# Folding the first feed-forward's low-rank factors into its weight tiles on chip

## The reference, cut to what matters

```python
def lora(x, w, a, b):            # rank 16, SCALING = 2.0
    return x @ w.T + (x @ a.T) @ b.T * 2.0
g = silu(lora(h, w1, A1, B1)) * lora(h, w3, A3, B3)    # w1, w3: 1376 x 512
x = x + lora(g, w2, A2, B2)                            # w2: 512 x 1376
```

## Time and profile before

| | |
|---|---|
| median of 3 runs | 2982.11 us (2981.08 to 2985.95) |
| the profiled execution's own time | 2981.35 us |
| its span on the core | 2979.5 us |
| PE busy | 2886.9 us, 97% of the span |
| DVE, ACT, POOL busy | 1705.7, 1121.6, 991.4 us |
| the stage (from 868 to 1102 us) | 234 us |

### The profile page before, as it was taken

How to read it: one execution, slowest core, us unless ns; L and a number is a source line. 1 busy time by engine, 2 the same in 40 slices (tenths; PEclk the granted TensorE clock), 3 DMA queues, 4 the chain that set the end, 5 groups by cost and what they waited for, 6 DMA issues and landing times.

```text
span 2979.5 us, 47771 instructions
## 1 busy us (share of the span) xinstructions
PE 2886.9 (97%) x16134; PEld 2433.1 (82%) x16134; DVE 1705.7 (57%) x3462; ACT 1121.6 (38%) x3635; POOL 991.4 (33%) x830
## 2 busy tenths in 40 slices
PE   7999999999999998899999999999999999999999
PEld 6888888888888865577778888888778888888787
DVE  6545544445462249988766666666664444445644
ACT  4322222222242237732354444444443333333432
POOL 3433343423313226644333322332232333332221
PEclk9999999999999999999999999999999999999999
DMA  3111111111112111011111101110021111110111
GB/s 121 46 50 41 40 39 41 48 41 44 42 36 57 34 43 30 27 43 39 37 40 36 31 26 32 35 35 18 26 60 33 36 35 35 35 35 22 46 50 46
DMA packets 68613, 120.09 MB, mean 40 GB/s; under 512 B 8681, under 2 KB 14185, under 8 KB 68113
## 3 DMA queue, kind: packets, MB, share of 16 engines
q1 hardware_dynamic: 68498, 118.60, 13.4%
HBM read 116.41 MB, written 2.10 MB: 40 GB/s over the span
## 4 chain that ended last, share of the span: by engine, by line
PE 86%; DVE 8%; issue 3%; ACT 2%; POOL 1%; DMA 0%; DVEq 0%; SPq 0%; ACTq 0%; POOLq 0%
PE proj L397 40%; PE outp L397 24%; PE heado L1015 6%; PE score L974 6%; PE turn L1001 3%; PE score L397 2%; PE proj L413 1%; PE proj L941 1%; DVE blockmax L1715 1%; DVE picks L1725 1%; PE outp L1995 0%; DVE firstmax L1723 0%; PE turn L924 0%; PE proj L1958 0%; DVE acts L1705 0%
## 5 line engine op out<-in xcount | busy, mean ns | idle before, releaser
L397 PE MATMUL outp<-w_out,acts 128*128 128x512 f32 x3288 | 843.2, 400 | 13.0 <-DVE x L1700 3.9
L397 PE MATMUL proj<-xnT,w_in 128*128 128x512 f32 x3192 | 757.2, 392 | 1.3 <-ACT big L1079 1.3
L397 PEld LDWEIGHTS outp<-w_out,acts 128*128 128x128 f32 x3288 | 594.1, 188 | 144.1 <-DVE x L1700 13.0
L397 PEld LDWEIGHTS proj<-xnT,w_in 128*128 128x128 f32 x3192 | 592.6, 188 | 124.7 <-issue 1.5
L397 PE MATMUL proj<-ctxT,w_kv 128*128 128x512 f32 x1536 | 366.0, 394 | 19.8 <-POOL w_kv L731 18.6
L729 POOL TENSOR_TENSOR w_out<-ring,consts 128x512 fp32r<-128x512 f32 x96 | 102.4, 1066 | 820.9 <-PE outp L397 820.9
L397 PEld LDWEIGHTS proj<-ctxT,w_kv 128*128 128x128 f32 x1536 | 286.6, 189 | 79.1 <-issue 18.6
L1306 DVE TENSOR_TENSOR x<-x,outp 128x512 f32<-128x512 f32 x360 | 244.7, 685 | 182.2 <-PE outp L397 179.1
L1082 DVE COPY big<-proj 128x512 f32<-128x512 f32 x136 | 93.6, 688 | 343.6 <-PE proj L397 339.3
L1079 ACT ACTIVATE big<-proj 128x512 f32<-128x512 f32 x136 | 81.4, 598 | 476.4 <-PE proj L397 469.7
L729 POOL TENSOR_TENSOR w_kv<-ring,consts 128x512 fp32r<-128x512 f32 x93 | 98.0, 1053 | 464.0 <-DMA ring<-in_L_wk 445.6
(11 more groups left out here) (330 smaller groups left out, 4022.7 us busy)
## 6 DMA issues: line engine op xcount, KB each, us to landing
ring<-in_L_wq SPq DMA_DIRECT2D x96, 256.0 KB, 2.7
ring<-in_L_wo SPq DMA_DIRECT2D x96, 256.0 KB, 2.7
ring<-in_F_in SPq DMA_DIRECT2D x52, 256.0 KB, 2.7
ring<-in_L_wk SPq DMA_DIRECT2D x48, 256.0 KB, 2.7
ring<-in_L_wv SPq DMA_DIRECT2D x48, 256.0 KB, 3.4
ring<-in_F_out SPq DMA_DIRECT2D x41, 256.0 KB, 2.6
x<-in_x SPq DMA_DIRECT2D x2, 1024.0 KB, 8.4
big<-in_ctxT SPq DMA_DIRECT2D x4, 512.0 KB, 8.0
```

What stands on the lines that cost most here:

```text
L397: mm = pe.matmul(bank_ap, w_ap(a, c), rhs(b, c), start=first and c == 0 and n == 0, stop=last and c == chunks - 1 and n == len(PASSES) - 1)
```

## The change: what it does

The low-rank products with activations go away. Instead the product of the factors themselves is made on PE, B1 A1 and B3 A3 for an `in` or `in2` tile and A2 B2 for an `out` tile. DVE adds twice that to the raw tile in its ring slot (`merge`), and ACT and POOL round and split the sum as they did the raw tile. The factors stand four times on 64 partitions (high, low, high, high against high, high, low, ...), so that one matmul over 64 rows gives all three passes and one more; `fold_in` makes both input tiles of the next chunk, with eight matmuls of 64 rows and 128 columns that alternate between partitions 0 to 63 and 64 to 127 and between two banks; `fold_out` makes the `out` tile's with one of 64 rows and 512 columns.

```diff
+        def fold_bank(n):
+            return proj[n] if n < 2 else ln_banks[n % 2]
+
+        def fold_in(pe, c):
+            m, n = F0.events, F0.tile(0, c, 0)
+            for k in range(2):
+                m.wait(pe, "merged", n + k - 1 if n else 0)
+            for i in range(DC):
+                for k in range(2):
+                    rows = slice(64 * k, 64 * k + 64)
+                    mm = pe.matmul(fold_bank(n + k)[:, i * P:(i + 1) * P], low_in[rows, i * P:(i + 1) * P],
+                                   low_b[rows, 0, c * P:(c + 1) * P], start=True, stop=True)
+                    if i == DC - 1:
+                        mm.then_inc(m["folded"], 1)
+
+        def fold_out(pe, c):
+            m, n = F0.events, F0.tile(0, c, 2)
+            if c == 0:
+                m.wait(pe, "a_split", 1)
+                pe.wait_ge(b_split, 5)
+            m.wait(pe, "merged", n - 1)
+            pe.matmul(fold_bank(n)[:, :], low_a2[:, c * P:(c + 1) * P], low_b2[:, :], start=True, stop=True).then_inc(m["folded"], 1)
+
+        def merge(dve, n):
+            m, r = F0.events, n % F0.ring
+            m.wait(dve, ("landed", r), 16 * (n // F0.ring + 1))
+            m.wait(dve, "folded", n + 1)
+            dve.scalar_tensor_tensor(ring[:, r, :], fold_bank(n)[:, :], 2.0, ring[:, r, :], ALU.mult, ALU.add).then_inc(m["merged"], 1)
...
         def pe_tail(pe, n, out_of):
+            if F0.stage == n:
+                pe.wait_ge(b_split, 4)
+                for i in range(2):
+                    LA[0].events.wait(pe, ("pfree", i), LA[0].projections * NG)
+                fold_in(pe, 0)
             for b in range(B):
+                if F0.stage == n and b == B - 1:
+                    F0.events.wait(pe, "merged", 2)
...
-            for F in (F0, F1):
+            if F1.stage == n:
+                low_rank_product(pe, F1, 0)
+            for F in (F0, F3):
                 if F.stage == n:
-                    low_rank_product(pe, F, 0)
...
                 deviations(b)
+                if F0.stage == n and b == 2:
+                    ffn_act_first(act, F0)
...
                 add_of(b)
+                if F0.stage == n and b in (1, 2):
+                    merge(dve, b - 1)
...
+            if j == 0:
+                dve.wait_ge(b_landed, 48)
                 for raw, cols in pieces:
-                    dve.tensor_copy(low_b[rows, i, cols], raw[rows, :]).then_inc(b_high, 1)
+                    dve.tensor_copy(low_b[:, 0, cols], raw).then_inc(b_high, 1)
...
-                dve.memset(low_b[others, i, :].bitcast(F32), 0.0).then_inc(b_high, 1)
...
+                    if A.kind == "silu" and c == 0:
+                        LA[0].events.wait(sp, "pv", 2 * NH)
+                        for dst, src in A.small:
+                            sp.dma_start(dst, src).then_inc(m["small_landed"], 16)
...
-            ffn_pool_tiles(pool, A, 0, 0)
+            ffn_pool_tiles(pool, A, 0, 0, IN_TILES if A.kind == "silu" else None)
             if A.kind == "silu":
                 m.wait(pool, "small_landed", 32)
...
+                pool.tensor_tensor(low_a2[:, :], a2_raw, consts[0:64, C_ZERO:C_ZERO + 1].broadcast_to([64, 11 * P]), ALU.add)\
+                    .then_inc(m["a_high"], 1)
+                m.wait(pool, "a_high", 1)
+                pool.tensor_tensor(low_a2[32:64, :], a2_raw[32:64, :], low_a2[32:64, :].bitcast(F32), ALU.subtract)\
+                    .then_inc(m["a_split"], 1)
...
+                        if A.kind == "silu" and half == int(opened):
+                            fold_out(pe, c)
                     if A.kind == "silu":
-                        if not first:
-                            second_low(*((g, j - 1) if j else (g - 1, GH - 1)))
+                        if c < A.chunks - 1:
+                            fold_in(pe, c + 1)
                         m.wait(pe, "split", A.tile(g, j, 1) + 1)
...
+            if A.kind == "silu":
+                m.wait(act, "merged", A.tile(g, j, k) + 1)
...
                     if A.kind == "silu":
+                        for n in range(3 * c + 2, min(3 * c + 5, 3 * A.chunks)):
+                            merge(dve, n)
```

More of the change, by code:

```diff
@@ L575, in take_low_part @@
             cols = slice(half * HALF, (half + 1) * HALF)
[L576 to L582, removed]
@@ L1508, in ffn_pe @@
             pre = int(A.low_rank)
[L1510 to L1514, removed]
-                    if c == 0:
-                        m.wait(pe, "a_split", 1)
-                    for k in range(2):
-                        mm = pe.matmul(ln_banks[half][0:96, :], low_a2[:, c * 96:(c + 1) * 96],
-                                       acts[:, j, k, half * HALF:(half + 1) * HALF], start=c == 0 and k == 0,
-                                       stop=c == A.chunks - 1 and k == 1)
-                    mm.then_inc(m["lowfull"], 1)
             def out_product(p, slots, bs, last):
@@ L1535, in out_product @@
                     m.wait(pe, "added", B * p + (b - 1))
-                    more = last and A.kind == "silu"
                     if opened and b < 2:
@@ L1539, in out_product @@
                     else:
-                        mm = pe_out(pe, b, slots, last=not more)
-                    if more:
-                        if b == 0:
-                            m.wait(pe, "low2_low", 2)
-                            m.wait(pe, "a_split", 2)
-                        mm = pe.matmul(outp[b % 2][:, :], low_in[0:96, b * S:(b + 1) * S], low_b2[:, :], start=False, stop=True)
+                        mm = pe_out(pe, b, slots)
                     mm.then_inc(m["outfull"], 1)
@@ L1656, in chunks @@
                     more = not (isinstance(c, int) and c == A.chunks - 1)
-                    for what in A.what[:-1] if more else ():
+                    for what in A.what[:-1] if more and A.kind != "silu" else ():
                         ffn_act_high(act, A, *after(g, j), what)
@@ L1669, in chunks @@
                            .then_inc(m["pfree", half], 1)
-                    if more:
+                    if A.kind == "silu":
+                        ffn_act_high(act, A, g, j, "out")
+                        for what in IN_TILES if more else ():
+                            ffn_act_high(act, A, *after(g, j), what)
+                    elif more:
                         ffn_act_high(act, A, *after(g, j), "out")
@@ L1767, in ffn_dve @@
             p = (A.chunks - 1) // 2
-            for half in range(2 if A.kind == "silu" else 0):
-                m.wait(dve, "low2", half + 1)
-                cols = slice(half * HALF, (half + 1) * HALF)
-                dve.scalar_tensor_tensor(low_in[64:96, cols], ln_banks[half][64:96, :], 2.0,
-                                         low_in[64:96, cols].bitcast(F32), ALU.mult, ALU.subtract)\
-                   .then_inc(m["low2_low"], 1)
             def last_add(b):
@@ L2542, in _ @@
             LA[0].events.wait(sp, "split", LA[0].tiles * NG)
-            LA[0].events.wait(sp, "pv", 2 * NH)
             ffn_sp(sp, F0)
```

162 lines of the change are left out of this document (67 added, 95 removed).

## The result

The changed kernel takes 3007.84 us (median of 4 runs, 3004.62 to 3009.82) against 2982.06 before: ratio 1.0083, 95% interval 1.0071 to 1.0095. It is 25.8 us slower, where 6.7 us less was predicted. Its profiled execution has a span of 3006.6 us, 27.1 more than the one of before.

What follows compares the result with a forecast made beforehand. PE, busy for 159.00 of 159.00 us in the middle of the changed stage, was taken as the bound. Gains of 29.4 us less costs of 22.7 gave net 6.7, from 2982.11 to 2975.4 us; range 2967.5 to 2981.5.

Steps and rivals of the forecast that it cites:

- the rows do pair: Against the rival that `fold_in`'s matmuls in two row halves don't pair: 4.7 us more, 2980.1 us; chance 0.25.
- POOL does collide: Against the rival that POOL doesn't hold up DVE's chain in the normalisation: 7.4 us back, 2968.0 us; chance 0.17.
- late weights: Rival: in some eight short chunks PE waits for weights; 0.9 us each ends the gain, 1.8 gives 2989; chance 0.07.
- Collision on POOL: In the normalisation ahead, POOL's long operations hold up DVE's `rstd` chain: 8.9 us instead of 2.46, 6.4 later.
- Clock behind the idle time: After PE's idle of about 7 us ahead of the stage, a low-clock stretch: 1.0 us added, between 0 and 2.
- fold_in: On PE in the changed stage, eight small matmuls running in pairs: 0.8 us each time, 8.8 us for 11.
- fold_out: On PE in the changed stage, a lone small matmul with changes of tile: 0.51 us each, 5.6 us for 11.
- Stall in chunk 0: `fold_in` stands directly behind `fold_out` and waits for DVE's merge between them: 0.9 us.
- The first `fold_in`: Ahead of out products of which one waits for DVE, so part hides behind that wait: 0.4 us taken back.
- Preparation of `low_b`: Loses a 1.23 us memset ahead of an attention product PE waits for: 0.8 us saved, between 0 and 1.5.
- Slack of the weights: In the changed stage, the preparation of `in2` tiles keeps ahead of PE with about 1.3 us to spare.
- The closing: From `second_low`'s last start to the next `rstd`, 9.6 us becomes 6.0: 3.6 saved, 0.9 of it counted among removed matmuls.

Runs made afterwards that it cites:

- N = 8: The changed kernel with 8 one-column memsets more on DVE, spread over the changed stage's chunks, which nothing reads: 2976.3 us, ratio 0.9982 to the kernel before.
- rstd in PSUM: The changed kernel with 8 idle DVE memsets, and small operands of the changed stage's `rstd` chain in PSUM instead of SBUF: 2970.57 us, ratio 0.9965.
- the other order: The changed kernel with 8 idle DVE memsets, `fold_in` doing four matmuls of one row half, then four of the other: 2975.24 us, ratio 0.9979.

## Why the prediction was wrong, point by point

**The step that failed** is none of the sum's terms but what the sum left out: it was made over the edits and the stages that they touch, and put the rest of the program at nothing, without a reason. A program's later part has a place in the engine's code, and 59 instructions more on DVE moved a loop to one of its 7 bad places. Worth 32.1 us in the trace and 31.5 in the medians (3007.84 against 2976.3). None of my rivals held it: the rows do pair, POOL does collide, and the only rival on the slower side, late weights at 0.07, didn't come. For the range to hold it, it would have needed one rival more: a loop of more than 256 instructions on DVE, its place shifted, 7 in 128 by what the runs showed, some 5 in 100 (an estimate that holds if the blocks are of 128).

**The sum itself** held. At the next stage's `rstd` the changed kernel is 5.4 us ahead where 6.7 was forecast; and the run with N = 8 is 0.18% faster than before by its ratio, 5.4 us, and 4.4 us by the spans of the profiled executions. The terms add up in the trace as well. From the last attention product ahead of the stage (866.42 before, 866.63 after) to the first `proj` products the changed kernel takes 2.1 us more, which is 7.6 of costs (7.8 forecast: 6.4, 1.0 and 0.8 less 0.4) less 5.5 for 24 matmuls; from there to the last out products it takes 4.7 less (5.6 forecast), and behind them 3.0 less (3.6 forecast): 5.6 in all, less the 0.2 that it was behind at the start.

- *Collision on POOL*: forecast a chain of 8.9 us, measured 8.7, with four operations through by the time POOL ended, as forecast. With rstd in PSUM the chain is 5.0 us shorter and the six matmuls 1.3, and the medians fell by 5.8. Of POOL's two operations, taken as 2.7 and 3.2 us, the first doesn't follow from the rows named for it (0.485 us for 176 elements would give 3.9); they took 2.53 and 3.15.
- *Clock behind the idle time*: forecast 1.0; the six matmuls alone took 1.27 us longer, at 1.2 GHz. Too low, though inside the bounds.
- *fold_in*: forecast 0.8. In the timeline, from 916.54 to 917.67 there are 1.13 us for two full matmuls (0.46) and the fold, and 0.1 more goes before the full pace is back: 0.79. Right in size; the reason given for it fell with the other order.
- *fold_out*: forecast 0.51. 1.41 less 0.79 leaves 0.62, 1.2 us more over 11. The changes of tile cost more on a lone small matmul than the earlier trace rows gave.
- *Stall in chunk 0*: forecast 0.9, measured 0.95 us of idle time in the trace; taking it away gave back 0.57.
- *The first `fold_in`*: from 866.42 to 872.24 before, from 866.63 to 872.80 after, 0.35 us more where 0.8 less 0.4 was forecast.
- *Preparation of `low_b`*: forecast 0.8. PE's wait there went from 1.32 to 1.07 us, but the changed kernel comes to the stage 0.2 us behind, not 0.8 ahead (866.63 against 866.42). PE's `score` products near 61 us, ahead of all that the change touches on PE, start between 60.50 and 62.31 us in ten of the kernels run, so 0.8 can't be told here.
- *Slack of the weights*: held; PE is busy for 159.00 of 159.00 us.
- *The closing*: 3.6 us less was forecast, 9.6 to 6.0. The last out products start at about 1089.04 (three matmuls ahead of the end of a row of 51 that begins at 1077.94), 6.6 us ahead of the next `rstd`: 3.0 less.
- *Matmuls removed*: not measured apart. From the first `proj` products to the last out products it is 196.1 us before (895.34 to 1091.47) and 191.4 after (897.63 to 1089.04), 4.7 less; 88 matmuls of 0.228 less the folds as measured above and the stall give 4.4.

**Between 1102 us and attention 2** the lead shrinks by 2.2 us. The windows from 1200 to 1300 us, after and before (the same clock time, so the work in them is shifted by some 5 us):

```profile
1200.00:1300.00 100.00, 88.70 (x547) 63.14 (x546) 84.69 (x160) 67.23 (x172) 50.89 (x43) 0.92 0.10 30
```

```profile
1200.00:1300.00 100.00, 85.52 (x580) 59.33 (x576) 88.04 (x166) 68.36 (x180) 57.16 (x50) 1.00 0.09 29
```

The granted clock is 0.92 against 1.00, stretches at 1.2 GHz in a stage where PE has many short idle times. But that number scatters from run to run: 0.97 in three of the four kernels made of the one before by memsets, 1.00 in the fourth, 0.92 to 0.97 in the eight made of the changed one. Whether the change has a share in it is open.

## What to carry to other kernels

Count DVE's instructions ahead of every loop, and in it: here a loop of 264 was made slower by an edit in another stage ahead of it, and a single idle operation more put it right. By blocks of 128 a loop of up to 257 would, as an estimate, lie in three of them wherever it starts; no run tried that, nor a loop of another engine. If a kernel that should be faster isn't, align both traces by the same operations before explaining anything: here the changed stage had given what was forecast, and all of the loss sat 570 us behind it. Small operations on DVE that stand on the path beside long ones on POOL are better off with an operand in PSUM: 3.7 us for the chain instead of 8.7.

## What the runs showed of the hardware that I had not expected

- At a jump back of the loop of 264 instructions DVE stands still for 0.5 to 0.6 us at the good starting places and for 5.0 to 6.8 us at the bad ones (all jumps of six runs): one pause of 3.1 to 4.3 us at the loop's first instruction and one of 1.1 to 3.0 us where its first border is. The bad places came back after 128 and 256 instructions.
- The page shows it in one number, the transfers of queue 14, of kind "instruction": 48 to 50 against 73 to 77.
- Matmuls in different halves of PE's rows, and in different banks, ran beside each other though four of one half stood first in the code.
